# Spectral layer: TensorE's eight turns over pairs of filters, written out within an image in place of a loop

## What is computed

```python
def _compute_spectral(u, sigma, phi, Mpp, Mpm):
    U_plus, U_minus = _stu_conv(phi, u, PADDED_SL)
    s = sigma ** SIGMA_POW
    out = jnp.einsum('btkd,k,kde->bte', U_plus, s, Mpp)
    out = out + jnp.einsum('btkd,k,kde->bte', U_minus, s, Mpm)
    return out
...
for i, frac in enumerate((1, 2, 4, 8)):
    xi = x[:, :T // frac]
    si = _stu(xi, sigma, phi, M_u[i], M_phi_plus[i], M_phi_minus[i])
...
return jnp.sum(stacked * weights, axis=-1)
```

## Time and profile before

| | us |
|---|---|
| median of 3 runs | 7840.03 (7836.26 to 7846.94) |
| the profiled execution | 7841.85 |
| its span, first to last instruction | 7839.8 |
| TensorE matrix products busy (share of the span) | 7046.8 (90%) |
| weight loads | 6018.8 (77%) |
| VectorE | 6238.0 (80%) |
| ScalarE | 4510.7 (58%) |
| GpSimd | 4630.3 (59%) |

### The profile page before, as it was taken

The page is one execution under the profiler, slowest core; times in us unless marked ns, Lnnn a source line. Parts: engine busy times, 40 slices in busy tenths (PEclk is TensorE's granted clock), DMA queues, the critical chain, the costliest instruction groups (busy, mean ns, idle before and its releaser), DMA issues. The chain is left out here.

```text
span 7839.8 us, 179804 instructions
## 1 busy us (share of the span) xinstructions
PE 7046.8 (90%) x64572; PEld 6018.8 (77%) x64572; DVE 6238.0 (80%) x9093; ACT 4510.7 (58%) x9442; POOL 4630.3 (59%) x5010
## 2 busy tenths in 40 slices
PE   8999989999899998999857999798978989899898
PEld 6888768887688876888747888456658878888888
DVE  7999879998799987999846776455667878788787
ACT  5888658886588866887612333244444544444444
POOL 5888658886588865888647765121124444444444
PEclk9999999999999999999979999899989999999999
DMA  2333223332233322333267775000024333334343
GB/s 65 91 93 90 80 61 90 93 91 79 61 90 93 92 79 62 90 93 92 77 201 228 223 198 166 6 14 22 11 73 123 111 120 111 119 111 129 101 129 99
DMA packets 595211, 775.58 MB, mean 99 GB/s; under 512 B 52215, under 2 KB 528408, under 8 KB 592193
## 3 DMA queue, kind: packets, MB, share of 16 engines
q1 hardware_dynamic: 542529, 594.11, 25.6%
q0 software_dynamic: 51840, 169.91, 7.6%
HBM read 730.16 MB, written 33.66 MB: 97 GB/s over the span
## 5 line engine op out<-in xcount | busy, mean ns | idle before, releaser
L647 POOL TENSOR_TENSOR l_arena<-l_arena 128x768 f32<-128x768 f32 x1536 | 2589.2, 1686 | 451.5 <-DVE l_arena L579 445.1
L579 DVE TENSOR_TENSOR_SCAN l_arena<-l_arena,psum 128x772 f32<-128x772 f32 x1536 | 2662.4, 1749 | 176.8 <-PE psum L406 74.5
L500 ACT ACTIVATE l_arena<-l_arena,l_A 128x384 f32<-128x384 f32 x3072 | 1643.0, 603 | 38.2 <-DVE l_arena L579 32.8
L408 PE MATMUL psum<-l_arena 128*128 128x128 f32 x11520 | 1499.8, 280 | 46.4 <-DVE l_arena L579 42.6
L408 PEld LDWEIGHTS psum<-l_arena 128*128 128x128 f32 x11520 | 1367.9, 193 | 169.9 <-issue 146.1
L419 PE MATMUL psum<-l_ident,l_arena 128*128 128x128 f32 x9216 | 1257.6, 273 | 50.5 <-ACT l_yT L506 41.6
L419 PEld LDWEIGHTS psum<-l_ident,l_arena 128*128 128x128 f32 x9216 | 1055.1, 141 | 60.2 <-POOL l_arena L647 60.2
L2641 POOL TENSOR_TENSOR st_U<-st_Uc,st_U 128x384 f16<-128x384 f32 x512 | 469.3, 917 | 970.7 <-ACT st_U L2607 970.7
L1211 POOL DMA_INDIRECT l_G<-neighbours,l_idx x648 | 622.0, 960 | 391.2 <-issue 188.9
L490 ACT ACTIVATE l_arena<-l_arena,l_BT 128x256 f32<-128x256 f32 x1728 | 746.7, 496 | 7.5
L2457 PE MATMUL psum<-st_U,st_W 128*128 128x128 f16 (+3 forms) x6144 | 532.0, 229 | 32.5 <-POOL st_U L2641 23.1
(11 more groups left out here) (456 smaller groups left out, 11910.2 us busy)
## 6 DMA issues: line engine op xcount, KB each, us to landing
l_arena<-c_rows SPq DMA_DIRECT2D x1536, 192.0 KB, 3.0
st_FS<-filter_sums SPq DMA_DIRECT2D x128, 1155.0 KB, 9.6
st_F<-filter_parts SPq DMA_DIRECT2D x128, 320.5 KB, 6.7
neighbours<-l_xt SPq DMA_DIRECT2D x256, 72.0 KB
st_mab<-in_st_mp SPq DMA_DIRECT2D x68, 256.0 KB, 9.2
st_mab<-in_st_mm SPq DMA_DIRECT2D x68, 256.0 KB, 6.8
l_G<-neighbours,l_idx POOLq DMA_INDIRECT x648, 3.7
l_arena<-in_x SPq DMA_DIRECT2D x4, 1152.0 KB, 5.2
```

Source lines behind the costliest of these rows:

```text
L408: mm = pe.matmul(ps[:, o:o + P], dtuT[:, g % 2, t, h * P:(h + 1) * P], diagB[:, rank[s] % 3, t, :], start=True, stop=True)
L500: act.activation(decay[:, s % NDC, half(h)], dtv[:, g % 2, h, :], ACT.Exp, scale=A[:, g // NRC, h, n:n + 1]).then_inc(s_exp, 1)
L579: dve.tensor_tensor_scan(hbuf[:, n, run], decay[:, s % NDC, run], x2_ps[s % 2][:, run], 0.0, ALU.mult, ALU.add).then_inc(s_scan, 1)
L647: pool.tensor_tensor(hC[:, s % NHC], halves(hbuf[:, s % NS, :]), Cs[:, s % NCS, :].unsqueeze(1).broadcast_to([P, 2, RC]), ALU.mult).then_i ...
```

## The change

TensorE's loop is replaced by a Python `for`, so that the eight turns of an image stand one after the other in its program. The loop over images (L2301) stays a loop, and so do the loops of the other four engines. What TensorE computes, its order and its waits are as they were.

```diff
-                    with pe.Fori(0, KF // 2 - 1) as i:
-                        filters_pair(i, False)
-                    filters_pair(KF // 2 - 1, True)
+                    for i in range(KF // 2):
+                        filters_pair(i, i == KF // 2 - 1)
```

## The result

The changed kernel took 7711.8 us (median of 4 runs, 7708.55 to 7712.44) against 7841.93 us for the kernel before (4 runs, 7836.26 to 7846.94). The ratio is 0.983, with a 95% interval of 0.982 to 0.985: 130 us less, where 137.5 were forecast.

A forecast was written before the change was run, and what follows sets the result against it. TensorE was taken to be the bound, idling for instructions after 24 taken jumps. The profiled 7841.85 us less 137.5 gave 7704.3, or 7702.5 us as a median after a 1.8 us correction; range 7693 to 7741 us.

The forecast's parts named there:

- What bounds the kernel: TensorE, busy for 90% of the span, lacks instructions in "issue" pauses before lines 2442 and 2422: 75.0 and 38.0 us.
- the taken jumps: TensorE's 24 jumps back over a turn, six in each of four images, cost 5.73 us each.
- The size, 137.5 us: Measured image times less jump-free ones of 420.64 us: 113.0 us of pauses plus 24.5 us, mainly products at low clock.
- the free stretch: Eight units across turns 6 to 7, where no jump is taken: 54.28 us, taken as a sample of every changed turn.
- a stretch without a pause longer than 54.3 us: Sign in the profile after, for eight units on TensorE, that would show the prediction wrong.
- Entry, fall-through, register work: Loop set-up and jump at each image's start, untaken branch at turn 6's end, and register instructions: all counted as nothing.
- Who is late next: TensorE's waits on GpSimd, VectorE and ScalarE, 2.0, 1.3 and 0.2 us over 99.7 us, were counted as already in 54.28.
- More program: Fetching the written-out turns on TensorE adds no traffic and no pauses at packet ends: zero cost.
- the slower rival: Fetch pauses wander into TensorE's straight program, 163 places at 1.65 us, 269 us lost: 7971 us; chance 0.04.
- Half of it stays: Rival: table loading at a turn's end causes the second pause, whose 38.0 us stay: 7740.5 us; chance 0.08 with its other case.
- Its other case: Another engine's own jump comes into the open at turn ends, leaving 75.0 us: 7777.5 us; within the 0.08 chance.
- The jump is not what pauses: Rival: pauses stay at turn ends and only branch instructions go: 7828 to 7840 us; chance 0.02.

The follow-up runs named there:

- the last two runs: Changed kernel with the mixing matrices' low parts moved from GpSimd to VectorE, 7693.5 us; then also VectorE's eight matrix operations dealt one to each place, 7636.6 us.

## Why the prediction was right, and where its size was off

*What bounds the kernel; the taken jumps.* Right: the pauses are the jumps, they go with their number, and none is left without them. The clock is 1.00 in every stretch, as forecast.

*The size, 137.5 us.* Of this 126.96 came. It is made up of the 113.0 us of pauses and of 37.9 us by which TensorE's busy time in the four images fell (1654.6 to 1616.7 us, the products that ran at the low clock), less 23.6 us by which its waits on GpSimd and VectorE grew: 127.3 us. The prediction had 24.5 us for the last two together, and they came to 14. The step that failed is "the stretch without a jump is thus a sample, four times over, of what every turn looks like in the changed kernel". The stretch of 54.28 us begins with unit 1 of turn 6, and that unit still stands in the shadow of the jump before turn 6: after a pause VectorE has caught up, TensorE does not wait for it, and the unit takes 6.51 us instead of 6.85. Two windows of eight units in the run with two turns in a body show it, the first from unit 1 of turn 2, right behind a jump, the second from unit 0 of turn 6, far from one:

```profile
6437.04:6491.33 54.29, 52.18 (x867) 50.11 (x865) 48.73 (x117) 29.19 (x60) 27.61 (x29) 1.00 0.35 100
...
6653.99:6708.63 54.64, 52.18 (x869) 50.13 (x865) 49.10 (x117) 29.18 (x60) 28.00 (x29) 1.00 0.46 132
```

The 28 stretches of the changed kernel are longer by 0.34 us each, 9.5 us, and the first one in an image by 0.2 more, 0.9 in all: 10.4 of the 10.55 us that are missing. The stretches of the earlier trace rows could have told it: by TensorE's timeline the last six units, 40.68 us, begin with one of 6.85 us, and the free stretch begins with the same unit at 6.51. One of the prediction's own signs of being wrong, a stretch without a pause longer than 54.3 us, thus came true, though the time lies inside the range.

*Entry, fall-through, register work.* Nothing, as forecast; the near jumps that were put back cost nothing either.

*Who is late next.* Named rightly (GpSimd, then VectorE, waits under 1 us), but counted as already in the 54.28, which held only part of them. The added ones come in the first two units of a turn and not at a turn's end. The jumps of the other engines, counted as nothing, cost the 0.9 us at the first change of turn. VectorE close to its limit was right too, and the last two runs show that it was the overlap with GpSimd and the uneven order that made it so.

*More program.* Right: no pause at any packet's end in eight turns in a row, so the slower rival has nothing. From 64.3 bytes an instruction the prediction read that "the bytes equal what is executed". In fact they held about two packets for each jump that the straight program does without.

*Half of it stays.* This rival rested on the loading of tables as the cause of the second pause. The runs with the head moved put that pause at the packet's end behind a jump. The loads may lengthen it there, but without the jump none of it is left. Its other case, another engine's jump in the open, has at most the 1.2 us that the run without three of their loops gained.

*The jump is not what pauses.* Fallen: without the far jumps no pause is left, and with 8, 16 or 24 of them as many first pauses come back.

## What to carry to other kernels

Look for idle time before matrix products that the trace puts down to "issue", at equal distances: the loop here, with a body of 1826 instructions, had them brought in anew and paid 5.3 us at every pass, and writing it out cost nothing, since in eight turns on end no wait for a packet shows. Where a loop must stay, the place of its head within a packet of instructions can be worth several us a pass. And take the sample for "without the stall" from a stretch that does not begin in the recovery from one, or the waits that the stall swallowed are missing from the sum.

## What the runs showed of the hardware that was not expected

The price of a far jump on TensorE depends on where the target lies: at a turn's end 3.5 us with 216 instructions left in the packet, 5.3 to 5.8 with 96, 9.0 with 28. With 28, sixteen jumps cost more (143 us) than twenty-four with 96 (127 us), and the kernel with fewer jumps is the slower one.

A 128 x 512 operation on VectorE took 0.68 us alone and 1.64 us beside a GpSimd operation of 1.61 us, a 128 x 384 one 0.54 and 1.51 us; one of this size with an operand in PSUM took 0.56 us beside a GpSimd operation of 0.94 us. The Trainium skill, "Advanced Engine Details and Errata", section "VectorE Performance Modes", says that VectorE's second port to SBUF is shared with GpSimd, so that GpSimd's instructions and VectorE's two-port ones interfere or block each other; the durations agree, though no run here shows the port itself.
